# Cross attention on one core: the order of logits, value products and transposes in a step, with weights in four places

## The reference

```python
q = (text_embeds @ Wq.T + bq).reshape(num_texts, num_words, HEADS, HEAD_DIM)
k = (video_embeds @ Wk.T + bk).reshape(num_vids, num_frames, HEADS, HEAD_DIM)
v = (video_embeds @ Wv.T + bv).reshape(num_vids, num_frames, HEADS, HEAD_DIM)
logits = jnp.einsum('avhd,bthd->abhvt', k, q) / math.sqrt(HEAD_DIM)
weights = jax.nn.softmax(logits, axis=3)
attn = jnp.einsum('avhd,abhvt->abhtd', v, weights)
attn = attn.mean(axis=0)
return attn @ Wo.T + bo
```

## Time and profile before

| | us |
|---|---|
| median of 3 runs (2425.32 to 2430.37) | 2425.41 |
| the profiled execution, its own time | 2424.38 |
| its span, first to last instruction | 2422.3 |
| attention loop, first to last reciprocal (L1868), 256 of them | 567.1 to 2108.1 |
| TensorE / VectorE / ScalarE / GpSimd busy over the span | 2112.0 / 2004.9 / 1674.1 / 1762.8 |

### The profile page before, as it was taken

The page is one execution under the profiler, slowest core; times in us unless marked ns, Lnnn a source line. Parts: engine busy times, 40 slices in busy tenths (PEclk is TensorE's granted clock), DMA queues, the critical chain, the costliest instruction groups (busy, mean ns, idle before and its releaser), DMA issues. The chain is left out here.

```text
span 2422.3 us, 50062 instructions
## 1 busy us (share of the span) xinstructions
PE 2112.0 (87%) x14341; PEld 1631.3 (67%) x14341; DVE 2004.9 (83%) x3388; ACT 1674.1 (69%) x4826; POOL 1762.8 (73%) x1672
## 2 busy tenths in 40 slices
PE   4555876838999999999999999999999999967993
PEld 2345766835777777777777777777777777657883
DVE  6977765147999999999999999999999999776664
ACT  2153211526888888888888888888888988704662
POOL 3643432755888888888888888888888888824773
PEclk9676665968999999999999999999999999957997
DMA  7421113622222222222222222222222222143555
GB/s 247 143 70 44 35 50 90 169 70 61 66 65 66 66 65 65 66 65 65 66 65 65 66 65 65 66 66 65 66 66 65 65 66 65 44 97 107 156 156 153
DMA packets 157684, 197.68 MB, mean 82 GB/s; under 512 B 33200, under 2 KB 99888, under 8 KB 155504
## 3 DMA queue, kind: packets, MB, share of 16 engines
q1 hardware_dynamic: 139280, 174.80, 26.6%
q0 software_dynamic: 8064, 16.60, 2.5%
q10 hardware_dynamic: 10208, 4.66, 0.7%
HBM read 77.58 MB, written 17.74 MB: 39 GB/s over the span
## 5 line engine op out<-in xcount | busy, mean ns | idle before, releaser
L1958 POOL TENSOR_TENSOR attend_weights<-attend_weights,attend_scales 128x512 f32<-128x512 f32 x1024 | 1047.1, 1044 | 198.4 <-DVE attend_scales L1868 198.4
L1842 DVE TENSOR_REDUCE attend_maxima<-attend_psL 128x16 fp32r<-128x1024 f32 x512 | 618.5, 1208 | 4.7 <-PE attend_psL L1757 2.7
L1915 ACT ACTIVATE attend_turned<-attend_psT 128x512 f32<-128x512 f32 x1024 | 554.0, 595 | 36.2 <-PE attend_psT L1776 12.9
L1776 PE MATMUL attend_psT<-consts,attend_weights 128*128 128x128 f32 x4096 | 553.9, 275 | 4.6 <-POOL attend_weights L1958 2.0
L1776 PEld LDWEIGHTS attend_psT<-consts,attend_weights 128*128 128x128 f32 x4096 | 474.0, 140 | 97.3 <-POOL attend_weights L1958 14.2
L1790 PE MATMUL attend_psA<-attend_turned,attend_value_ring 128*64 128x256 f32 x4096 | 498.5, 386 | 0.8 <-ACT attend_turned L1915 0.8
L1756 PE MATMUL attend_psL<-attend_key_ring,attend_q_high 128*128 128x512 f32 x1024 | 457.7, 447 | 3.9 <-ACT attend_weights L1908 2.3
L1908 ACT ACTIVATE attend_weights<-attend_psL,attend_maxima 128x64 f32<-128x64 f32 x2048 | 449.7, 354 | 4.7 <-DVE attend_maxima L1842 4.7
L1903 ACT ACTIVATE attend_weights<-attend_weights 128x512 f32<-128x512 f32 x512 | 342.3, 669 | 135.6 <-DVE attend_weights L1852 135.6
L1757 PE MATMUL attend_psL<-attend_key_ring,attend_q_low 128*128 128x512 f32 x1024 | 403.4, 394 | 0.0
L1852 DVE TENSOR_TENSOR attend_weights<-attend_psL,attend_maxima 128x512 f32<-128x512 f32 x512 | 354.2, 692 | 52.7 <-DVE attend_maxima L1842 2.0
(11 more groups left out here) (318 smaller groups left out, 2473.6 us busy)
## 6 DMA issues: line engine op xcount, KB each, us to landing
attend_key_ring<-keys SPq DMA_DIRECT2D x512, 128.0 KB, 2.2
attend_value_ring<-values SPq DMA_DIRECT2D x128, 256.0 KB, 2.5
moe2mix_w_tile<-in_L_ffn_w_dram SPq DMA_DIRECT2D x71, 256.0 KB
select_xbuf<-in_x_dram SPq DMA_DIRECT2D x16, 1024.0 KB, 5.5
moe1mix_w_tile<-in_L_ffn_W_dram SPq DMA_DIRECT2D x39, 256.0 KB
select_emb<-L_attn_video_embeds_dram ACTq DMA_DIRECT2D x16, 256.0 KB, 4.2
values_gates<-project_vg SPq DMA_DIRECT2D x8, 512.0 KB, 2.6
retain_vg<-values_gates SPq DMA_DIRECT2D x8, 512.0 KB
```

Source lines behind the costliest of these rows:

```text
L1776: mm = pe.matmul(psT[:, j % 2, k * P:(k + 1) * P], weights[:, 4 * parity + j, k * P:(k + 1) * P], ident, is_transpose=True, start=(k == 0) ...
L1842: dve.tensor_reduce(maxima[:, both, :].rearrange("p j v -> p (j v)"), psL[:, both, :].rearrange("p j (v f) -> p (j v) f", f=FR), X, ALU.ma ...
L1915: act.activation(turned[:, parity, :, h, t, :], psT[:, j % 2, :].rearrange("p (k q) -> p k q", k=SUB), ACT.Copy).then_inc(turned_copied, 1)
L1958: pool.tensor_tensor(w, w, scales[:, s, :, None].to_broadcast([P, VC, FR]), ALU.mult).then_inc(normalised, 1)
```

## The change

In the loop, TensorE's step becomes: S of n-1, L of all four units, X of n-3 (written as two halves in a row), then T of all four units of n-2. VectorE does both maxima and both subtractions of n, then the sums of n-1. ScalarE does E3 of n-1, C3 of n-3, E0 of n, C0 and C1 of n-2, E1 and E2 of n, C2 of n-2. GpSimd scales all four units of n-2 and then adds the halves of n; before, it scaled n-1 around that addition. The weights have four places: two in a buffer of their own and two in `hidden`, which is written to DRAM during the first block (`hidden_kept`, waited for at step 2) and read back into the two own places at the loop's end (`hidden_back`), where the output bias is then added.

Around the loop, the two routers' norms and the norm before the attention apply their result on ScalarE (`LayerNorm.apply`) from a `shift` that VectorE makes one batch later; the rows that come back from the first mixture are added by VectorE. Tables of rows in DRAM are stored with a partition's rows side by side ("(p g)"). The final addition and output no longer have a block of their own: SP waits for the last scatters and goes on within the expert block.

```diff
+    def statistics(self, dve, hidden, before=None):
+
+        for b in range(B + 2):
+            if b < B:
+                if before:
+                    before(b)
+                for g in range(b * TB, (b + 1) * TB):
+                    dve.bn_stats(self.stats[:, g, :], hidden[:, g, :]).then_inc(self.steps, 1)
+            if b > 1:
+                part = slice((b - 2) * TB, (b - 1) * TB)
+                dve.wait_ge(self.root_ready, b - 1)
+                dve.scalar_tensor_tensor(self.shift[:, part], self.mv[:, part, 0], -1.0, self.root[:, part], ALU.mult, ALU.mult).then_inc(self.shift_ready, 1)
+            if b < B:
+                part = slice(b * TB, (b + 1) * TB)
+                dve.wait_ge(self.steps, b * 2 * TB + TB)
+                for g in range(b * TB, (b + 1) * TB):
+                    dve.bn_aggr(self.mv[:, g, :], self.stats[:, g, :]).then_inc(self.steps, 1)
+                dve.wait_ge(self.steps, (b + 1) * 2 * TB)
+                dve.tensor_scalar(self.square[:, part], self.mv[:, part, 1], self.scale, self.eps, ALU.mult, ALU.add).then_inc(self.square_ready, 1)
+
...
+    def apply(self, act, hidden, rows, ready, b):
+
+        act.wait_ge(self.shift_ready, b + 1)
+        for g in range(b * TB, (b + 1) * TB):
+            ins = act.activation(rows[:, g, 0:D], hidden[:, g, :], ACT.Identity, bias=self.shift[:, g:g + 1], scale=self.root[:, g:g + 1])
+        ins.then_inc(ready, 1)
...
+                        for n in range(RING):
+                            sp.wait_ge(result_out[n], 16 * len(range(n, used, RING)))
+                        for q in range(PARTS):
+                            part = slice(q * QT, (q + 1) * QT)
+                            for k in range(2):
+                                tokens = K.result_dram[2][SPARE + k * N:SPARE + (k + 1) * N, :].rearrange("(p g) d -> p g d", p=P)
+                                sp.dma_start(back[:, k, part, :], tokens[:, part, :]).then_inc(back_in[q], 16)
+                        rows_out = out.rearrange("b (i p) d -> p (b i) d", p=P)
+                        for q in range(PARTS):
+                            part = slice(q * QT, (q + 1) * QT)
+
+                            sp.wait_ge(added, 2 * (q + 1))
+                            sp.dma_start(rows_out[:, part, :], K.hidden[:, part, :]).then_inc(stored, 16)
+                        sp.wait_ge(stored, 16 * PARTS)
...
         mixedT = qT
+        lower = sb("weights", [P, 2 * UNITS, KC])
+        upper = K.hidden[:].rearrange("p g d -> p (g d)").rearrange("p (s k) -> p s k", k=KC)
+        kept = K.hidden_dram.rearrange("p (s k) -> p s k", k=KC)
+        hidden_kept, hidden_back = sem("hidden_kept"), sem("hidden_back")
+
+        def weights_of(slot):
+
+            at = slot % 2 * UNITS
+            return (lower if slot < 2 else upper)[:, at:at + UNITS, :]
...
 
-        UNITS = 4
-        STEPS, FIRST, LAG = 2 * NKC, 8, 3
+        STEPS, FIRST, LAG, SLOTS = 2 * NKC, 8, 3, 4
...
+                    for b in range(B):
+                        sp.wait_ge(rows_added, b + 1)
+                        sp.dma_start(kept[:, b, :], upper[:, b, :]).then_inc(hidden_kept, 16)
...
+                    def add_rows(b):
+                        part = slice(b * TB, (b + 1) * TB)
+                        dve.wait_ge(back_in[b], 16)
+                        dve.tensor_tensor(K.hidden[:, part, :], K.hidden[:, part, :], back[:, part, :], ALU.add).then_inc(rows_added, 1)
+
+                    def added(b):
+                        if b == 0:
+                            add_rows(0)
+                        if b + 1 < B:
+                            add_rows(b + 1)
                         dve.wait_ge(rows_added, b + 1)
...
+                    norm.statistics(dve, K.hidden, added)
...
+                    sp.wait_ge(turned_ready, (B * STEPS - 2) * UNITS)
+                    for b in range(B):
+                        sp.dma_start(lower[:, b, :], kept[:, b, :]).then_inc(hidden_back, 16)
...
-                    def mix(n, q, k, run, first):
+                    def mix(n, q, k, run, first, part):
 
                         r, slot, parity = k % 2, k // 2, k % 2
-                        pe.wait_ge(values_in[slot], 16 * (q + 1))
-                        pe.wait_ge(turned_copied, 4 * n + (UNITS + 2))
-                        if first:
-
-                            pe.wait_ge(run_copied, run + 1)
...
+                            pe.wait_ge(turned_copied, 4 * n + (UNITS + 2))
+                            if first:
...
+                        if part == 1:
+                            mm.then_inc(chunks_mixed, 1)
...
+                            shift(n - 1, 1)
                         if exists(n):
                             if early == 0:
...
-                        if exists(n - 2):
-                            turn_weights(n - 2, k % 2, 0)
-                        if exists(n - LAG):
-                            before = quarter(i, p, q4 - 1) if k < LAG else q
-                            mix(n - LAG, before, (k - LAG) % 4, run, early == LAG)
-                        if exists(n):
-                            shift(n, 0)
                             logits(n, p, k, 1)
-                        if exists(n - 2):
-                            turn_weights(n - 2, k % 2, 1)
+                        for half in range(2):
+                            if exists(n - LAG):
+                                mix(n - LAG, before, (k - LAG) % 4, run, early == LAG, half)
+                        for pair in range(2):
...
+                        n = index(i, p, s)
                         if exists(n):
-                            maximum(n, 0)
-                            subtract(n, parity, 0, exists(n - 2))
+                            if isinstance(n, int) and n == 2:
+                                dve.wait_ge(hidden_kept, B * 16)
+                            for pair in range(2):
+                                maximum(n, pair)
+                                subtract(n, k, pair, exists(n - SLOTS))
+                            if isinstance(s, int) and s in (2, 4):
+                                low(1 - p, s // 2 - 1, (i * 2 + p) * 2 + (s // 2 + 2))
                         if exists(n - 1):
-                            total(n - 1, 1 - parity, 0)
-                            total(n - 1, 1 - parity, 1)
-                            invert(n - 1, 1 - parity)
-                        if exists(n):
-                            maximum(n, 1)
-                            subtract(n, parity, 1, exists(n - 2))
-                            if isinstance(s, int) and s in (1, 3):
-                                low(1 - p, s // 2, (i * 2 + p) * 2 + (s // 2 + 3))
+                            total(n - 1, (k - 1) % SLOTS, 0)
...
                         if exists(n - 1):
-                            exponentials(n - 1, 1 - parity, 1)
+                            exponentials(n - 1, (k - 1) % SLOTS, (3,))
+                        if exists(n - 3):
+                            copy_turned(n - 3, 1 - parity, (3,))
+                        if exists(n) and early in (2, 4):
+                            high(1 - p, early // 2 - 1, (i * 2 + p) * 2 + (early // 2 + 2))
+                        if exists(n):
+                            if isinstance(n, int) and n == 2:
+                                act.wait_ge(hidden_kept, B * 16)
+                            exponentials(n, k, (0,))
                         if exists(n - 2):
-                            copy_turned(n - 2, parity, 0)
+                            copy_turned(n - 2, parity, (0, 1))
                         if exists(n):
-                            exponentials(n, parity, 0)
+                            exponentials(n, k, (1, 2))
+                        if exists(n - 2):
+                            copy_turned(n - 2, parity, (2,))
                         if early == LAG - 1 and exists(n - LAG):
                             keep_run(i * 2 + (p - 1))
-                        if exists(n - 2):
-                            copy_turned(n - 2, parity, 1)
...
                         n = index(i, p, s)
-                        if exists(n - 1):
-                            normalise(n - 1, 1 - k % 2, 0)
+                        if exists(n - 2):
+                            normalise(n - 2, (k - 2) % SLOTS)
                         if exists(n):
-                            halve(n, k % 2)
-                        if exists(n - 1):
-                            normalise(n - 1, 1 - k % 2, 1)
+                            halve(n, k)
...
+                        if b == 0:
+                            pool.wait_ge(hidden_back, B * 16)
                         pool.tensor_tensor(rows, rows, K.bo_all[:, None, :].to_broadcast([P, TB, D]), ALU.add).then_inc(bias_added, 1)
 
                 @block.tensor
@@ -2001,7 +2045,8 @@
```

181 lines of the change are left out of this document (82 added, 99 removed).

## The result

The changed kernel takes 2531.81 us (median of 4 runs, 2530.22 to 2537.01), the kernel before 2426.98 (4 runs), a ratio of 1.0434 with a 95% interval of 1.0413 to 1.0454. The forecast was 2518 in a range of 2482 to 2550. The profiled executions are 2533.2 and 2424.38 us, their spans 2530.9 and 2422.3, so 108.6 us have to be accounted for.

What follows compares the result with a forecast made beforehand. VectorE bounds the kernel before at 5.97 us a step; the new order makes TensorE's circle 6.37. 2424.38 + 102 (loop) + 3 (run changes) + 2 (tail) - 8 (norm) - 6 (end) = 2517.4, so 2518, range 2482 to 2550.

Steps and rivals of the forecast that it cites:

- The bound: Attention loop: VectorE's queue sets 5.97 us a step; TensorE needs 5.7 to 5.8, so longer added waits lengthen every step.
- not slower: Rival, attention loop: TensorE keeps VectorE's pace at 5.97 us a step, total 2416 us; 4%.
- The place of the wait: TensorE's loop step: transposes of unit 3 wait for the second copy, starting 1.89 us after unit 0's instead of 1.3.
- the first circle: TensorE's loop step: shift, logits, value products and transposes, with waits for ScalarE's copies of units 0 and 1; 6.37 us.
- The step: Attention loop: 6.37 us a step, 0.40 more than 5.97, giving +102 us over 255 steps.
- Two circles of nearly the same length that don't add: Loop: one through TensorE, one through ScalarE's copies and exponentials to unit 3's logits; both 6.37 us, sharing value products and first copy.
- Run changes: Loop's eight run changes: projections and ScalarE's copy of the result fall on TensorE's circle; +3 us (0 to +8).
- Tail: Behind the loop's last logits: GpSimd scales a step later, up to four more instructions; +2 us (0 to +4).
- The norm: Norm before the attention: falls from 31.7 to 22 us; taken as -8 us (-10 to -2).
- The lock that was weighed there: Norm before the attention: VectorE's moved addition and GpSimd's root may exclude each other, giving back up to 1.0 us each.
- The clock rival: Attention loop: sixteen transposes together drop TensorE to the 1.2 GHz level; +1150 us, near 3670; 1%.
- Both circles adding up: Rival, attention loop: TensorE's and ScalarE's circles add part of each other; 6.7 us a step, 2602 us; 8%.

Runs made afterwards that it cites:

- max_half: The changed kernel with VectorE's maxima taken over half of the frames of each video; 2603.00 us on another chip, where the kernel before takes 2495.19.
- three_banks: The changed kernel with a third bank for transposed weights, and the later runs' projections and their additions left out; 2503.16 us.
- copy_half: The changed kernel with ScalarE copying only half of each bank of transposed weights, which the value products read twice; 2468.17 us.
- alternate: The changed kernel with TensorE's order all logits, half the value products, transposes of units 0 and 1, second half, transposes of units 2 and 3; 2457.86 us.
- exp_half: The changed kernel with ScalarE taking the exponential of only half the columns of units 1 and 2; 2529.15 us.
- shift_in_hole: The changed kernel with unit 3's shift moved between the transposes of units 0 and 1 and those of units 2 and 3; ratio 1.0368.
- places_only: The changed kernel with its four places and the save and return of `hidden`, but the old order on every engine; 2409.52 us.
- edges_only: The changed kernel with the old loop, two places of weights and the old order on all engines; 2411.55 us.

## Why the prediction was right, step by step

- The bound. Right: a wait on TensorE's queue lengthens every step, VectorE's floor of 5.97 is untouched, and `max_half` shows that it no longer counts. Too generous was the 5.7 to 5.8 us that TensorE's queue was to need without any wait. In the new order it needs 0.30 + 1.96 + 1.88 + 1.82 (`three_banks`) = 5.96, so there is nothing to spare against 5.97. The 5.7 to 5.8 stood outside the sum of 6.37 and did not harm it; the 5.96 leaves the rival "not slower" less room than its 4% assumed.
- The place of the wait. Transposes of unit 3 were to start 1.89 after those of unit 0, released by the second copy. Measured 1.92, 0.14 behind that copy's end. The bracket of 0.34 stands one unit earlier, at unit 2 and the first copy; both waits come out of the same two banks. From the first transposes to the shift 2.33 was forecast and 2.30 came. `copy_half` and `alternate` show that it is this wait; `exp_half` shows that on the changed kernel it is the first circle and not the second.
- The step. 6.37 was forecast, 6.44 came. The term that was mis-sized is the shift. It was put at 0.22, and behind the transposes it takes 0.30 to the first logits. The turn to the value products was counted (0.10) and is there (0.33 from the last logits, where two logits are 0.23 apart). The second turn, from the transposes to products of 512 columns, was left out of the sum, although show it: the first logits behind transposes take 1204.29 - 1203.98 = 0.31, 0.08 more than 0.23. The other terms are within 0.03 together: 6.37 + 0.08 + 0.02 - 0.03 = 6.44. 255 x 0.07 is 18 us.
- Two circles of nearly the same length that don't add: right. Freed of the first, the kernel goes at 6.37 to 6.40 (`three_banks`, `shift_in_hole`), and 6.37 was forecast. In the changed kernel itself the second has 0.16 to spare: the exponential of unit 3 ends at 1213.93 and that unit's logits start at 1214.15, where `three_banks` needs 0.05 between the two. Of the 0.16, 0.10 is the dearer start after a wait, which is paid only where this circle binds.
- Run changes: +3 forecast. Four steps at a change take 27.91 where 4 x 6.44 is 25.76, 2.15 more; before it was 25.99 and 23.88, 2.11 more. So they cost nothing new, though 2.64 each was to fall on the circle; why less does was not tried. Not foreseen were the steps in which TensorE's group of four begins again, 0.16 longer each, some 6 us in all, and 3.6 us less than before at the loop's end (the last step is 2.47 long in place of 5.59).
- Places and save of `hidden`: 0 forecast, none found (`places_only` is 2 us below `edges_only`). Tail +2, measured 2.7.
- The norm: 22 us forecast, 23.9 measured (516.11 to 539.97) in place of 31.7. It was to bring -8 and brought -7.0 at the first reciprocal. Routers' norms 0: measured with all of the second mixture +0.5. The end -6: measured -6.5, of which 4.1 are the missing block (2.38 from the last scatter to the first load in place of 6.49).
- The lock that was weighed there. VectorE's addition is 0.68 long with GpSimd's root beside it and 0.69 each for the first two, which have none, and the root is 1.41 beside an addition and 1.01 without one. The root begins 0.18 after the addition and overlaps it by 0.50 (519.03 to 519.53), and it is 0.40 longer. So GpSimd pays 0.4, and not VectorE up to 1.0. GpSimd's 0.4 is off the path: this root ends at 520.44, and VectorE takes it up at 522.23. The Trainium skill (SBUF — State Buffer, "Who interferes with whom") lists this pair as contending, with the one that issues first going on undisturbed; the trace agrees.
- The clock rival. Sixteen transposes in a row with a hole in them, and the granted clock stays 1.00, 2.4 GHz, over the loop.
- The range. The upper end of 6.50 us a step would be 6.55 with the 0.28 that it names for the turn in place of 0.10, and the sum of the upper ends leaves out the +5 of the save and the +3 of the routers' norms. Neither touches the forecast.
- Not slower (2416): excluded by the hole. Both circles adding up (2602): excluded by `exp_half`, which takes 0.43 from one of them and changes nothing.

Summed by stretches the forecast had -8 + 105 + 2 + 0 - 6 = +93, and the trace shows -7.0 + 118.9 + 2.7 + 0.5 - 6.5 = +108.6. The loop is the whole error.
